# Moving tiles between the blocks of the path stage of a graph network and expert kernel

## The reference

```python
x1 = x_nodes[src].reshape(-1, N_SEG, EXTENT)          # normalised node rows, one for each edge
x2 = x_edges.reshape(-1, N_SEG, EXTENT)               # 16 segments of 32 features
i1, i2, i3 = (path_indices[:, 0], path_indices[:, 1], path_indices[:, 2])
contrib = path_coeffs[None, :, None] * x1[:, i1, :] * x2[:, i2, :]
edge_out = zeros(x2.shape[0], N_SEG, EXTENT).at[:, i3, :].add(contrib)
out = zeros(n_nodes, OP_SIZE).at[dst].add(edge_out.reshape(-1, OP_SIZE))
```

## Time and profile before

| | |
|---|---|
| median of 3 runs | 276.57 us (276.3 to 276.63) |
| the profiled execution's own time | 278.61 us |
| its span, first to last instruction | 276.8 us |
| mean granted TensorE clock | 0.994 |
| PE busy | 264.2 us (95%) |
| DVE busy | 223.9 us (81%) |
| ACT busy | 166.9 us (60%) |
| POOL busy | 39.5 us (14%) |

### The profile page before, as it was taken

One profiled execution on the slowest core, in us unless ns is written; L12 is line 12 of the kernel. 1 busy time (PEld: TensorE's weight loads), 2 busy tenths in 40 slices (PEclk: granted clock), 3 DMA queues, 4 the chain that ended last, 5 costly groups with the idle time before them and its releaser, 6 DMA issues.

```text
span 276.8 us, 5669 instructions
## 1 busy us (share of the span) xinstructions
PE 264.2 (95%) x1639; PEld 185.3 (67%) x1639; DVE 223.9 (81%) x662; ACT 166.9 (60%) x341; POOL 39.5 (14%) x52
## 2 busy tenths in 40 slices
PE   6999999999998889999999999969999999999996
PEld 4666788886443779996678787755666664468633
DVE  5977664299657979999999999999999997755372
ACT  6921431011427479978887878399889829353260
POOL 4000150060007736662000000000000000000000
PEclk9999999999999999999999999988999999999999
DMA  6699990000014735656233000004444429000002
GB/s 208 222 409 410 437 404 17 0 4 1 36 39 117 197 111 149 163 155 182 76 107 125 2 0 2 2 19 153 155 152 153 150 81 344 36 2 2 2 0 76
DMA packets 12592, 33.91 MB, mean 123 GB/s; under 512 B 3345, under 2 KB 3602, under 8 KB 12306
## 3 DMA queue, kind: packets, MB, share of 16 engines
q1 hardware_dynamic: 10482, 26.73, 26.7%
q0 software_dynamic: 2080, 6.82, 8.8%
HBM read 32.50 MB, written 1.05 MB: 121 GB/s over the span
## 4 chain that ended last, share of the span: by engine, by line
PE 85%; DVE 6%; ACT 3%; issue 3%; DMA 1%; DVEq 1%; ACTq 1%; SPq 0%
PE psum L1345 15%; PE psum L1294 15%; PE psum L1248 10%; PE psum L1348 8%; PE psum L1272 5%; PE psum L1277 4%; PE psum L1300 3%; PE psum L1419 3%; PE psum L1445 3%; PE psum L1191 3%; PE psum L1177 2%; PE psum L1336 2%; PE psum L1131 2%; DVE big L1039 2%; PE psum L1229 1%
## 5 line engine op out<-in xcount | busy, mean ns | idle before, releaser
L605 ACT ACTIVATE prod<-edges,coef_b 128x320 f32 (+1 forms) x78 | 43.2, 591 | 16.0 <-PE psum L1348 8.1
L1294 PE MATMUL psum<-big,dst_oh 128*128 128x512 f32 x108 | 50.6, 593 | 0.2 <-DVE big L1039 0.2
L1345 PE MATMUL psum<-prod,ident 128*128 128x128 f32 x160 | 31.8, 292 | 0.8 <-DVE prod L1029 0.7
L1029 DVE TENSOR_TENSOR prod<-big,prod 128x320 f32<-128x320 f32 (+1 forms) x53 | 29.2, 552 | 2.7 <-ACT prod L605 1.7
L1345 PEld LDWEIGHTS psum<-prod,ident 128*128 128x128 f32 x160 | 24.5, 190 | 10.3 <-issue 9.5
L1294 PEld LDWEIGHTS psum<-big,dst_oh 128*128 128x128 f32 x108 | 18.7, 191 | 14.7 <-issue 14.3
L1248 PE MATMUL psum<-edges,big 128*128 128x256 f32 x128 | 28.3, 380 | 0.0
L1248 PEld LDWEIGHTS psum<-edges,big 128*128 128x128 f32 x128 | 24.1, 190 | 3.5 <-issue 0.3
L1039 DVE TENSOR_TENSOR big<-big,prod 128x64 f32 (+2 forms) x80 | 26.3, 329 | 0.0
L605 ACT ACTIVATE xparts<-edges,coef_b 128x320 f32 (+1 forms) x48 | 25.7, 586 | 0.8 <-PE psum L1345 0.8
L470 POOL DMA_INDIRECT big<-xn_rows,big x16 | 16.9, 1054 | 33.0 <-DMA xn_rows<-xn 23.5
(11 more groups left out here) (223 smaller groups left out, 530.6 us busy)
## 6 DMA issues: line engine op xcount, KB each, us to landing
big<-in_w SPq DMA_DIRECT2D x3, 2048.0 KB, 16.4
edges<-in_edge SPq DMA_DIRECT2D x1, 3584.0 KB, 24.1
edges<-in_f SPq DMA_DIRECT2D x7, 512.0 KB, 3.4
edges<-in_edge SPq DMA_DIRECT2D x1, 2560.0 KB, 23.8
edges<-in_edge SPq DMA_DIRECT2D x5, 512.0 KB, 3.6
edges<-in_f SPq DMA_DIRECT2D x1, 2560.0 KB, 10.0
big<-in_f SPq DMA_DIRECT2D x4, 512.0 KB, 3.5
big<-in_gnn_w SPq DMA_DIRECT2D x1, 1024.0 KB, 6.0
```

What stands on the lines that cost most here:

```text
L605: nc.scalar.activation(slot(n)[:, 0:BLOCKS[b], :], segment(edges_of(b), single_column(words, p)), ACT.Copy, scale=coef_b[:, p:p + 1]).then ...
L1029: nc.vector.tensor_tensor(v, segment(xg[:, 0:tiles, :], first_column(words[b], p)), v, ALU.mult).then_inc(mults, 1)
L1294: last = mm(bank[2 + h], dst_oh[:, n % DR, h * P:(h + 1) * P], tile_sums(b, t), start=False, stop=False)
L1345: last = mm(path_sums(to), ident[:], product[:, 0:PT].rearrange("p t u -> p (t u)"), start=False, stop=True, skip_group_check=True)
```

## The change

The blocks become 10, 12 and 12 tiles, and KEPT becomes 8, 6 and 6. So the third block also has six tiles summed by TensorE, in six banks, and VectorE adds six tiles in each of the last two blocks (8 and 6 before). ScalarE's clears of the third block's `rest_sums` go; GpSimd clears them in one instruction after its gathers, in a room of their own. SLOTS is 13. After the last path 12 tiles are scattered, four as fp32 and eight split; KEPT_AT becomes 2, so the six copies of kept sums come in one go. The transfers of f1 also wait for the first block's scatters. Places in SBUF move accordingly.

```diff
-    BLOCKS = [10, 14, 10]
-    FIRST = [0, 10, 24]
-    KEPT = [8, 6, 4]
+    BLOCKS = [10, 12, 12]
+    FIRST = [0, 10, 22]
+    KEPT = [8, 6, 6]
...
-    SLOTS = 12
-    OWN_SLOTS, XN_SLOTS, PART_SLOTS = 5, 2, 3
+    SLOTS = 13
+    OWN_SLOTS, XN_SLOTS, PART_SLOTS = 5, 2, 4
...
-    SPLIT = 7
+    SPLIT = 8
...
-        kept_sums = [sum_room[0][:, 0:KEPT[0], :], x1g[1][:, 0:KEPT[1], :], sum_room[0][:, 0:KEPT[2], :]]
-        rest_sums = [sum_room[0][:, KEPT[0]:, :], sum_room[1], sum_room[0][:, KEPT[2]:, :]]
+        kept_sums = [sum_room[0][:, 0:KEPT[0], :], x1g[1][:, 0:KEPT[1], :], late_edges[:, 0:KEPT[2], :]]
+        rest_sums = [sum_room[0][:, KEPT[0]:, :], sum_room[1], edges[:, 0:BLOCKS[2] - KEPT[2], :]]
...
             sp.dma_start(ctrl_sb, rows(ctrl)).then_inc(ctrl_in, 16)
             w = f1.shape[1] // 2
+            sp.wait_ge(scattered, FIRST[1])
             for i in range(2 * KC):
...
             gather_rows(2)
+            pool.wait_ge(mults, NP)
+            nc.gpsimd.memset(rest_sums[2], 0.0).then_inc(cleared[2], 1)
...
-                if b == 2 and p == 0:
-                    act.wait_ge(scattered, FIRST[1])
-                    for i in range(BLOCKS[b] - KEPT[b]):
-                        nc.scalar.activation(rest_sums[b][:, i, :], zero_b[:, 0:1].broadcast_to([P, D]), ACT.Copy)\
-                            .then_inc(cleared[b], 1)
...
-                    dve.wait_ge(cleared[b], (1, 2, BLOCKS[b] - KEPT[b])[b])
+                    dve.wait_ge(cleared[b], (1, 2, 1)[b])
```

More of the change, by code:

```diff
@@ L112, in graph_and_experts @@
         xn_rows = nc.dram_tensor("xn_rows", [N, D], F32, kind="Internal").ap()
-        big = sb("big", [P, (2 * BLOCKS[0] + BLOCKS[1] + BLOCKS[1] - KEPT[1]) * D + T * STEP_W // 2 + 2 * T + 3 * NP])
+        big = sb("big", [P, (BLOCKS[2] + BLOCKS[1] + BLOCKS[1] - KEPT[1] + BLOCKS[0]) * D + T * STEP_W // 2 + 2 * T + 3 * NP])
         prod = sb("prod", [P, OWN_SLOTS, BMAX, U])
@@ L164, in graph_and_experts @@
         take = carve(big[:, :])
-        x1g = [take([BLOCKS[0], D]), take([BLOCKS[1], D])]
+        late_edges = take([BLOCKS[2], D])
+        x1g = [late_edges[:, 0:BLOCKS[0], :], take([BLOCKS[1], D])]
         late_sums = take([BLOCKS[1] - KEPT[1], D])
@@ L184, in edges_of @@
         def edges_of(b):
-            lo = FIRST[b] if b < NB - 1 else 0
-            return edges[:, lo:lo + BLOCKS[b], :]
+            return edges[:, FIRST[b]:FIRST[b] + BLOCKS[b], :] if b < NB - 1 else late_edges
         take = carve(late)
@@ L215, in graph_and_experts @@
         w_cat = take([KC, G + EX])
-        take = carve(x1g[0].rearrange("p t f -> p (t f)"))
+        take = carve(sum_room[0].rearrange("p t f -> p (t f)"))
         f1_parts = [take([KC // 2, f1.shape[1]])]
-        ctrl_sb = take([KC, ES])
+        f2_parts = [take([2, D])]
+        ctrl_sb = carve(edges[:, BLOCKS[2] - KEPT[2]:BLOCKS[0], :].rearrange("p t f -> p (t f)"))([KC, ES])
         take = carve(edges[:, BLOCKS[0]:LATE, :].rearrange("p t f -> p (t f)"))
         f1_parts.append(take([KC // 2, f1.shape[1]]))
-        f2_lo = take([6, D])
+        f2_parts.append(take([4, D]))
         f2_hi = carve(late)([FC - 6, D])
-        take = carve(big[:, BLOCKS[0] * D:])
+        take = carve(big[:, :])
         xnT2 = take([KC, N])
@@ L319, in f2_sb @@
         def f2_sb(c):
-            return f2_lo[:, c, :] if c < 6 else f2_hi[:, c - 6, :]
+            return f2_parts[0][:, c, :] if c < 2 else f2_parts[1][:, c - 2, :] if c < 6 else f2_hi[:, c - 6, :]
         x_in, idx_in, w_in, w1_in, w3_in, w2_in = (sem(n) for n in
@@ L422, in _ @@
                 sp.wait_ge(mults, NP * (NB - 1) + 44 + 3 * i)
-                sp.dma_start(f2_lo[:, i:i + 2, :], rows(f2)[:, i:i + 2, :]).then_inc(f2_in, 16)
+                sp.dma_start(f2_parts[0] if i == 0 else f2_parts[1][:, i - 2:i, :], rows(f2)[:, i:i + 2, :]).then_inc(f2_in, 16)
             sp.wait_ge(mults, NP * NB)
@@ L1017, in multiply @@
                     if direct(b, 0):
-                        dve.wait_ge(edge_in[b], 16)
+                        dve.wait_ge(edge_in[b], 16 if b < NB - 1 else 16 * (BLOCKS[b] // 2))
                 v = slot(n)[:, 0:tiles, :]
```

## The result

The changed kernel takes 290.98 us (median of 4 runs, 289.46 to 291.19) against 276.44 us before. The ratio is 1.051, 95% interval 1.049 to 1.054: 5% slower. The forecast was 291.7 us.

What follows compares the result with a forecast made beforehand. VectorE and TensorE were taken as neck and neck, with TensorE the bound after the change: +0.2 (third block's start) + 11.9 (its paths and scatters) + 3.0 (end) = +15.1 us, from 276.57 to 291.7 us; range 288.5 to 294.7.

Steps and rivals of the forecast that it cites:

- Second block, TensorE keeps its own cycle: Second block: TensorE's work unchanged, 4.56 us per six paths and a scatter; last sums done 2.8 us earlier.
- The hand-over: Between second and third block: TensorE idle 2.7 us for two late copies, clock loss 1.4 us; spends the 2.8 won.
- Third block: 64 TensorE paths at 0.475 instead of 0.222 us, 12 scatters instead of 14: 51.0 us against 39.1, +11.9.
- The end: After the last path: four fp32 tiles scattered instead of three, eight split instead of seven: +3.0 us; ScalarE's copies hidden.
- What lies beside: Work off the path: GpSimd's 2.7 us clear hidden; ScalarE's lost clears and the 13th slot counted 0.
- the warming matmuls: Third block, between paths: 31 added matmuls; counted at 0.053 us a path in the sum that prices by columns.
- removing ScalarE's clears: ScalarE's six clears of the third block's sums, 3.22 us: their loss counted 0, as VectorE was never idle then.
- they do not wait for it, they only lose their lead: Between second and third block: VectorE and ScalarE go on until the 13 slots are full while TensorE stands still.
- the rival that the clock holds: Between second and third block: full clock after TensorE's idle stretch, -1.4 us, 290.3 us; chance 14%.
- VectorE setting the pace: Third block: TensorE finds room and VectorE binds at 0.74 us a path; -1 us, 275.6 us; chance 3%.
- the price by columns: Third block: narrow matmul costs by its columns, 0.387 us a path, +9.5 us in all, 286.1 us; chance 5%.
- the clock stays low longer: Clock low longer between the blocks, or ScalarE's feed visible at the end: +1.5 to +3, up to 294.7 us; together 16%.

Runs made afterwards that it cites:

- a: Changed kernel with all six copies of the second block's sums together behind path 5 (REST_LEAD 6 instead of 11): 286.97 us.
- i: The changed kernel, unaltered, run once more on another chip: 292.18 us, where the kernel before took 278.76.
- d: Changed kernel with four instead of six kept tiles in the third block, so no second or warming matmuls there: 284.55 us.
- b: Changed kernel without the 31 warming matmuls between the third block's paths: 287.74 us.
- e: Changed kernel with ScalarE's six clears of the third block's sums put back and GpSimd's clear removed: 296.13 us (before 278.71 there).
- j: Changed kernel with ScalarE's six clears put back and GpSimd's clear removed, a second run: 295.02 us (before 278.76 there).
- h: Changed kernel with four kept tiles in the third block and the second block's copies behind path 10 instead of 5: 282.39 us.
- g: Changed kernel without the third block's second and warming matmuls, sums of two tiles left out: 282.70 us (before 278.71 there).
- k: Changed kernel without the third block's second and warming matmuls, all six copies behind path 10: 278.78 us (before 278.76 there).
- c: Changed kernel with five instead of six kept tiles in the third block, its second matmul 32 columns wide: 289.82 us.

## Why the prediction was right

In the order of its steps, each from the profiles; the sum of the measured ones is the difference of B - A, 14.7 us.

- *Second block, TensorE keeps its own cycle.* Forecast 2.8 us earlier than before. Measured from A to the end of the last path's sums: 179.0 - 126.15 = 52.85 us, before 184.18 - 128.46 = 55.7, so -2.9.
- *The hand-over.* Forecast: four clears, an idle stretch of 2.7 us, a clock at half speed for about 3 us; 7.8 us from the last path to the effective start of the next, now 4.8. Measured: idle 2.38, clock 0.52 over 3.4 us, 185.83 - 179.0 = 6.8 us to the first path and some 0.7 more lost on the first paths (a's row of the first path is 3.3 us earlier, its B - A 4.0 less), 7.6 in all; before had 189.00 - 184.18 = 4.8, so +2.0 up to the first path. Run a shows that the wait and the clock account for 4.0 us together. That the clock falls is not certain, though: the same 2.38 us left it up in i.
- *Third block.* Forecast 51.0 us against 39.1. Measured 237.44 - 185.83 = 51.6 (with the 0.7 of the clock), before 228.06 - 189.00 = 39.1: +12.55. This is the main term. The price of the second matmul, taken from the second block's pair of paths, held to 1%, since shape and neighbours were the same.
- *The end.* Forecast +3.0. Measured 253.63 - 237.44 = 16.19 against 241.26 - 228.06 = 13.20: +2.99. ScalarE's six copies in a row stayed hidden.
- *What lies beside.* GpSimd's clear 2.66 us, hidden, as forecast.

-2.9 + 2.0 + 12.55 + 2.99 = 14.6, and the forecast sum was 15.1.

The comparison of TensorE's starts (189.2 against 189.0) treats both kernels alike, and that they are not. Before the change VectorE set the end of the third block: it was busy 38.44 of 39.00 us, TensorE's last scatters waited for its last add, and it had begun with the block 5.4 us ahead of TensorE's first path:

```profile
183.57 0.48 DVE L1029 TENSOR_TENSOR xparts<-edges,xparts 128x320 f32<-128x320 f32 x1
```

On the chip of runs a to d, three runs of before at a clock of 1.000 took 276.30 to 276.58 us and three at 0.994 took 276.18 to 276.30: a fallen clock cost it nothing. In the changed kernel TensorE is the bound, and the same fall costs 1.5 us.

That the forecast came within 0.7 us of the median has a share of luck. On the chip of run i the same kernel was 13.4 us above before and on the first 14.5, and how often the clock falls decides about 1.5 us.

Four statements in it did not hold, without moving the result. First, the warming matmuls were counted at their full 0.107 us in the comparison with the rivals; they cost 0.055 each (b). The main sum did not suffer, since it used the pair's measured 0.95 us. Second, removing ScalarE's clears was counted at 0, "VectorE was never idle then". In the changed kernel they would have delayed the copies, and so TensorE: their removal is worth 3 us (e, j). The sum did not suffer, because its time line lets the copies begin at 181.5 us, right behind the last sums at 181.4, and that holds only without the clears. The right question was not who waited before, but who would be waiting at that place after. Third, "they do not wait for it, they only lose their lead": VectorE starved 4.2 us at the hand-over, because ScalarE waited ahead of its scales. While TensorE is the bound this costs nothing; in d it was on the path (h). Fourth, the rival that the clock holds was a matter of the single execution and not of the kernel: one run of four of the changed kernel is that case, at 289.46 us, 1.5 below the others, against 1.4 forecast.

The rivals' fate: VectorE setting the pace (the faster side) is out by the windows and, for its price, by g and k; the price by columns is out by c; the clock that holds is the case of i. That the clock stays low longer did not happen in the changed kernel (0.52 over 3.4 us); it did in e and j. The tail's feed from ScalarE stayed hidden. On the Trainium skill's page "TensorE: Matmul & The Clock Gate": by its section "LDWEIGHTS (loading the stationary operand)" a weight load in ns takes about its columns over 1.2. An estimate from that figure: 107 ns for 128 columns, and a path of two fp32 matmuls, which are four instructions, has four of them; four times 107 is 0.43 us, near the 0.445 of run b, whatever the narrow matmul's columns. The traces of b and c agree with that reading; that the weight loads are the cause was not tried by itself.

Two things stay open. Why the clock falls behind an idle stretch of 2.38 us in some executions and not in others was not tried; the runs only show both. And the stall of the first block, on some chips and not on others, was only read; before has no profile from a chip without it.

No version of the change beats before. The fastest that leaves nothing out, h, takes 282.39 us against 278.71. Its B - A is 5.1 us above before's. Of these 3.0 are the two more tiles behind the last path, and 1.1 a fallen clock in that profile, if its run at 1.000 (281.67 us, the profiled one 282.77) is taken as the measure.

## What to carry to other kernels

Moving work between two engines that are both near full has to be costed on each of them alone, from rows of the same shape: 4 us were to be won on VectorE, and TensorE paid 12.6 for the third block alone. Here a second fp32 matmul of 64 columns cost as much as one of 128 (0.445 us a path with either), and halving its columns once more gave back about 0.015 us a path (c): in a stream like this, price the instructions and not the columns, from a row with the same neighbours. And when more PSUM banks are used in a block, look at where in the copying engine's order those banks' copies stand: here the two new ones stood five scales too late, for 2.4 us of idleness and, by chance of the execution, 1.5 us of clock.

## What the hardware showed that was not expected

- A warming matmul between a narrow and a wide one filled 0.06 of its own 0.11 us: from the wide matmul's start to the next start was 0.22 us behind it and 0.28 without (b).
- A narrow fp32 matmul of 32 columns took 0.14 us where one of 64 took 0.17, and the wide one behind it 0.30 instead of 0.28 (c).
- The same idle stretch of 2.38 us left the granted clock at 0.52 for 3.4 us in one execution and at 1.00 in another, a difference of 1.5 us in the time (changed and i). In the second the clock had been down at 99 to 103 us already; whether that matters was not tried.
- The clock also fell without an idle stretch of that kind. In k no gap of TensorE's was longer than 0.29 us from 222.0 to 225.5, where it was busy 2.45 of 3.50 us, and the clock was 0.50 from 226 to 228. In g the same end of the paths (226.0 to 229.5, again 2.45 of 3.50 us) left it at 1.00.
- Before took 276.3 us on some chips and 278.7 on others, and the difference goes with one stall of ScalarE and TensorE some 5 to 9 us into the path stage: the profiles of a to d lack it and start the copies at 126.1 us, those of e to k have them start at 127.6 to 128.4.
